# Eight gathered blocks and both edge counts moved into layer 0's first stage

## What is computed

```python
def _gat(x, W, a_src, a_dst, b, src, dst):
    xl = (x @ W).reshape(N, HEADS, C)                    # 4 heads of 32
    al = jnp.einsum('nhc,hc->nh', xl, a_src)
    ar = jnp.einsum('nhc,hc->nh', xl, a_dst)
    e = leaky_relu(al[src] + ar[dst], 0.2)
    m = segment_max(e, dst); w = exp(e - m[dst])
    alpha = w / (segment_sum(w, dst)[dst] + 1e-16)
    return segment_sum(xl[src] * alpha[..., None], dst).reshape(N, HEADS * C) + b

fwd = _gat(layernorm(x), W_f, ..., src, dst)
bwd = _gat(layernorm(x), W_b, ..., dst, src)
```

## Time and profile before

| | |
|---|---|
| median of 3 runs | 5654.59 us |
| the profiled execution | 5651.35 us |
| its span | 5649.4 us |
| instructions | 49583 |
| TensorE busy | 2856.7 us (51%) |
| VectorE busy | 3808.5 us (67%) |
| ScalarE busy | 1462.3 us (26%) |
| GpSimd busy | 3287.9 us (58%) |
| mean granted TensorE clock | 0.73 |

### The profile page before, as it was taken

One profiled execution on the slowest core, in us unless ns is written; L12 is line 12 of the kernel. 1 busy time (PEld: TensorE's weight loads), 2 busy tenths in 40 slices (PEclk: granted clock), 3 DMA queues, 4 the chain that ended last, 5 costly groups with the idle time before them and its releaser, 6 DMA issues. The chain is left out here.

```text
span 5649.4 us, 49583 instructions
## 1 busy us (share of the span) xinstructions
PE 2856.7 (51%) x13052; PEld 2230.7 (39%) x13052; DVE 3808.5 (67%) x6115; ACT 1462.3 (26%) x2526; POOL 3287.9 (58%) x3284
## 2 busy tenths in 40 slices
PE   7513200000000000016799987888888888884777
PEld 5412200000000000015577633777777767773456
DVE  7357778886454555546643464999999998995753
ACT  1113333332233333311222222222222222221220
POOL 0267777777777777754440233777777777772200
PEclk9655555555555555557799998999999999996888
DMA  3133344432363333334232345999999999993114
GB/s 101 36 83 108 102 136 148 132 101 87 103 220 110 110 109 105 106 92 129 87 125 68 101 185 208 314 319 330 322 323 326 321 326 323 322 326 100 67 49 148
DMA packets 288659, 961.78 MB, mean 170 GB/s; under 512 B 77678, under 2 KB 118259, under 8 KB 246896
## 3 DMA queue, kind: packets, MB, share of 16 engines
q0 software_dynamic: 169728, 483.60, 28.1%
q1 hardware_dynamic: 118784, 476.59, 25.4%
HBM read 626.03 MB, written 345.69 MB: 172 GB/s over the span
## 5 line engine op out<-in xcount | busy, mean ns | idle before, releaser
L1249 PE MATMUL e_psE<-e_we,e_eaT 128*128 128x256 f32 x3136 | 899.9, 413 | 268.3 <-DVE e_wv L1148 141.9
L1111 POOL DMA_INDIRECT e_kv<-kv,rec x784 | 875.8, 1117 | 256.1 <-issue 238.2
L779 POOL DMA_INDIRECT g_g<-t,rec x784 | 776.0, 990 | 250.6 <-issue 250.3
L779 POOL DMA_INDIRECT g_g<-t,dst_of x784 | 742.5, 947 | 260.2 <-issue 258.0
L1249 PEld LDWEIGHTS e_psE<-e_we,e_eaT 128*128 128x128 f32 x3136 | 647.1, 209 | 388.9 <-ACT e_eaT L1192 288.5
L1407 PE MATMUL j_psM<-ident,tail 128*128 128x128 f32 x32 | 7.5, 429 | 1148.5 <-PEq L53 1148.5
L1250 PE MATMUL e_psE<-e_kv,ident 128*128 128x256 f32 x1568 | 508.1, 408 | 0.0
L1407 PEld LDWEIGHTS j_psM<-ident,tail 128*128 128x128 f32 x32 | 7.0, 330 | 1149.3 <-issue 1149.3
L816 DVE TENSOR_TENSOR_SCAN g_wv<-g_fx,g_wv 128x2176 f32<-128x2176 f32 x98 | 459.0, 4684 | 0.4 <-issue 0.4
L1118 POOL DMA_INDIRECT e_q<-q,q_of x392 | 370.5, 945 | 119.4 <-issue 119.4
L956 ACT ACTIVATE g_st<-g_wv 128x2048 f32<-128x2048 f32 x98 | 375.8, 3835 | 0.0
(11 more groups left out here) (516 smaller groups left out, 6533.6 us busy)
## 6 DMA issues: line engine op xcount, KB each, us to landing
state<-e_st SPq DMA_DIRECT2D x98, 1088.0 KB, 6.2
e_ea<-in_edge_attr SPq DMA_DIRECT2D x98, 896.0 KB, 9.5
state_f<-g_st SPq DMA_DIRECT2D x49, 1088.0 KB, 4.3
state_b<-g_st SPq DMA_DIRECT2D x49, 1088.0 KB, 4.3
m_work<-xs SPq DMA_DIRECT2D x119, 128.0 KB, 2.2
ys<-m_work SPq DMA_DIRECT2D x119, 128.0 KB, 1.7
xs<-g_ta SPq DMA_DIRECT2D x28, 512.0 KB
g_g<-t,rec POOLq DMA_INDIRECT x784
```

The lines of the kernel that those rows point to most:

```text
L779: pool.indirect_dma_start(g[:, u, j, :], None, tab, bass.IndirectOffsetOnAxis(ap=at_, axis=0)).then_inc(gat[u], 16)
L1111: pool.indirect_dma_start(kv[:, u, b, :], None, c.kv, bass.IndirectOffsetOnAxis(ap=c.rec[:, t, 1:2], axis=0)).then_inc(gkv[u][b // 4], 16)
L1249: nc.tensor.matmul(half, eaT[:, m, j, k, :], we[:, k, :], start=(k == 0), stop=False)
```

## The change

- **First stage.** VectorE's memsets are cut to the padding, and the strip of x is cleared by GpSimd. SyncE loads the weights ahead of x, the attention vectors with four DMAs in place of sixteen, and x in seven column groups with a semaphore each. TensorE folds the weights ahead of the counts; 6 counts go ahead of the tables and 1 lies in each group; 85 follow the tables. Then come 98 counts of the sources (a second bank, `psS`), 54 of them ahead of the work of `target_logits`, which is a helper inside this stage now, and 44 behind it. Both segments' ends are made here (`ends_of(k, ...)`). The records are stored behind the tables.
- **Gathers ahead.** Once the tables are stored, GpSimd gathers the first row per partition and the blocks 0 to 4, then issues the 49 scatters, then gathers blocks 5 to 7. The buffers are a ring of nine: five slots lie in `c.x`, four in `c.gx`.
- **The rank pass** has a reload and regather at its end, under its flag.
- **`graph_passes`** starts at block 8 on GpSimd and waits for a slot nine blocks back. Its counts and segments' ends are gone. The sort's row phases are in blocks 1 to 9, its turns in 10 to 30; SyncE writes and rereads the sorted keys at 34, VectorE unpacks them at 36 and makes the source logits ahead of block 48. The 49 scatters are issued at block 16.
- **`join_tails`** of layer 0 clears the strip of x on GpSimd and reloads x on SyncE, which waits for it.

The diff, cut to its core:

```diff
+RB, RING, RING_X = 16, 9, 5
+EARLY, BEFOREHAND = 5, 8
...
+def ring_slot(c, u):
+    if u < RING_X:
+        return c.x[:, u * (RB * TW):(u + 1) * (RB * TW)].rearrange("p (j w) -> p j w", j=RB)
+    return c.gx[:, u - RING_X]
+def gather_forward(c, pool, blocks, landed_of):
+    for blk in blocks:
+        for j in range(RB):
+            t = blk * RB + j
+            pool.indirect_dma_start(ring_slot(c, blk)[:, j, :], None, c.t1, bass.IndirectOffsetOnAxis(
+                ap=c.key[:, 1, t:t + 1], axis=0)).then_inc(landed_of(blk), 16)
+def target_logits(c, v, landed, first_in, values_in):
+    nc = c.nc
+    nc.vector.tensor_copy(c.lastkey[:, 0:1], c.key[:, 0, T - 1:T])
+    nc.vector.memset(c.sep[:, 0:1], 0.0)
+    nc.vector.tensor_tensor(c.sep[:, 1:T], c.key[:, 0, 1:T], c.key[:, 0, 0:T - 1], ALU.is_equal)
+    v.wait_ge(landed, first_in)
+    v.wait_ge(values_in, 16)
+    nc.vector.tensor_copy(c.ar[:, 0, :], c.first[:, 132:136])
+    v.drain()
+    for h in range(4):
+        nc.vector.tensor_tensor_scan(c.ar[:, :, h], c.sep[:], c.ar[:, :, h], 0.0, ALU.mult, ALU.add)
+    v.drain()
+    nc.vector.tensor_scalar(c.sep[:], c.sep[:], 1.0, BIG, ALU.subtract, ALU.mult)
+    v.drain()
...
-            AHEAD, EACH = 28, 10
-            assert AHEAD + NG * EACH == NBLK
+            names = ("L0_gnn_a_src_f", "L0_gnn_a_dst_f", "L0_gnn_a_src_b", "L0_gnn_a_dst_b")
+            AHEAD, EACH, BEFORE_VALUES = 6, 1, 54
...
+                x = A["x"]
+                rows = x[0:whole, :].rearrange("(p i) d -> p (i d)", i=NI)
+                for g in range(NG):
+                    if g == 3:
+                        sp.wait_ge(padded, 1)
+                    if g == 0:
+                        sp.dma_start(c.x[P - 1:P, 0:pad], x[whole:N, :].rearrange("(p i) d -> p (i d)", p=1)).then_inc(last_x_in, 16)
+                        for at, name in enumerate(names):
+                            with nc.allow_non_contiguous_dma("one word per partition"):
+                                sp.dma_start(avcol[:, at:at + 1], A[name].rearrange("h (c a) -> (h c) a", a=1)).then_inc(av_in, 16)
+                    for p0, p1 in slices_of(0, P - 1):
+                        sp.dma_start(c.x[p0:p1, g * GT * D:(g + 1) * GT * D],
+                                     rows[p0:p1, g * GT * D:(g + 1) * GT * D]).then_inc(x_in[g], 16)
...
+                sp.wait_ge(scattered, 16 * NI)
+                sp.dma_start(c.ar[:], c.st[0][0:EP, :].rearrange("(p t) w -> p t w", p=P)).then_inc(values_in, 16)
+                sp.wait_ge(bd, 2)
+                for q in range(2):
+                    sp.dma_start(c.ends[1][q].rearrange("(p l) -> p l", l=LO), ends[:, 1, q, :]).then_inc(wr, 16)
...
-                nc.vector.memset(key[:], N)
+                nc.vector.memset(key[96:128, :, E - full:T], N)
                 nc.vector.memset(nxt[:], N).then_inc(kz, 1)
-                nc.vector.memset(c.x[96:128, :], 0.0).then_inc(padded, 1)
...
+                v.wait_ge(last_x_in, 16)
+                for g in range(NG):
+                    v.wait_ge(x_in[g], 32)
+                    layernorm_stats(c, v, w, lambda j: c.x[:, (g * GT + j) * D:(g * GT + j + 1) * D], GT, vin, root, g + 1)
+                    if g:
+                        v.wait_ge(tr, g * GT)
+                    for j in range(GT):
+                        nc.vector.tensor_scalar(xln[:, j, 0:D], c.x[:, (g * GT + j) * D:(g * GT + j + 1) * D], w["mv"][:, j, 0:1],
+                                                w["rstd"][:, j:j + 1], ALU.subtract, ALU.mult).then_inc(xr, 1)
+                    for n in counted_with(g):
+                        count(n)
...
+                ends_of(0, psH)
+                for n in range(NBLK, NBLK + BEFORE_VALUES):
+                    count(n)
+                target_logits(c, v, first_in, 16, values_in)
+                for n in range(NBLK + BEFORE_VALUES, 2 * NBLK):
+                    count(n)
...
+                weights()
...
+                pe.wait_ge(vs, 1)
+                nc.tensor.matmul(psV[:, 0:1], c.one[:, 0:1].to_broadcast([P, P]), viol[:, 1:2], start=True, stop=True)
+                for n in rest:
+                    count(n)
+                counted(0, psH)
+                for n in range(NBLK, 2 * NBLK):
+                    count(n)
+                counted(1, psS)
...
+                nc.gpsimd.memset(c.x[96:128, pad:NI * D], 0.0).then_inc(padded, 1)
...
+                pool.wait_ge(kld, 112)
+                pool.wait_ge(stored[0], 32 * (NG // 2 + 1))
+                pool.wait_ge(stored[1], 32 * (NG // 2))
+                c.alone(pool)
+                pool.indirect_dma_start(c.first[:], None, c.t1, bass.IndirectOffsetOnAxis(ap=key[:, 0, 0:1], axis=0)).then_inc(first_in, 16)
+                gather_forward(c, pool, range(EARLY), lambda blk: c.gat[blk])
...
+                gather_forward(c, pool, range(EARLY, BEFOREHAND), lambda blk: c.gat[blk])
...
-        HB, FIRST, TURNS = 6, 18, 27
-        PHASES = ((1, 2, 3), (4,), (5,), (6,), (7,), (8,), (9,), (10,))
+        FIRST, TURNS, KEYS_OUT, SCATTER, COPIES = 1, 10, 34, 16, 18
+        PHASES = ((1, 2), (3,), (4,), (5,), (6,), (7,), (8,), (9,), (10,))
...
+                if 0 <= blk - COPIES < 16:
+                    others += copy_attributes(blk - COPIES)
+                if blk == SCATTER + 4:
+                    sp.wait_ge(scattered, NI * 16)
+                    sp.dma_start(ar_b[:], c.st[1][0:EP, :].rearrange("(p t) w -> p t w", p=P)).then_inc(logits_in, 16)
...
-            for blk in range(NB):
-                u = blk % U
-                if blk == HALF:
+            for blk in range(BEFOREHAND, NB):
+                u = blk % RING
+                if blk == SCATTER:
                     pool.wait_ge(starts_in, 32)
                     c.alone(pool)
                     for i in range(NI):
                         pool.indirect_dma_start(c.st[1], bass.IndirectOffsetOnAxis(ap=startn[:, i:i + 1], axis=0),
                                                 logit[:, i, :], None).then_inc(scattered, 16)
+                if blk == HALF:
                     pool.wait_ge(unpacked, 1)
                     c.alone(pool)
                     pool.indirect_dma_start(first[:], None, c.t2, bass.IndirectOffsetOnAxis(
-                        ap=c.src_of[:, 0:1], axis=0)).then_inc(first_in, 16)
-                if blk >= U:
-                    pool.wait_ge(used, blk - U + 1)
+                        ap=src_of[:, 0:1], axis=0)).then_inc(first_in, 16)
+                if blk >= RING:
+                    pool.wait_ge(used, blk - RING + 1)
                     c.alone(pool)
                 for j in range(G):
                     t = (blk % HALF) * G + j
-                    at_, tab = (c.rec[:, t, 1:2], c.t1) if blk < HALF else (c.dst_of[:, t:t + 1], c.t2)
-                    pool.indirect_dma_start(g[:, u, j, :], None, tab, bass.IndirectOffsetOnAxis(ap=at_, axis=0)).then_inc(gat[u], 16)
+                    at_, tab = (c.key[:, 1, t:t + 1], c.t1) if blk < HALF else (dst_of[:, t:t + 1], c.t2)
+                    pool.indirect_dma_start(ring_slot(c, u)[:, j, :], None, tab,
+                                            bass.IndirectOffsetOnAxis(ap=at_, axis=0)).then_inc(gat[u], 16)
 
         @block.vector
...
+                if blk == KEYS_OUT + 2:
+                    unpack()
+                if blk == HALF - 1:
                     source_logits()
...
+def reload_rows(c, sp, rows_padded, rows_in):
+    x, whole = c.A["x"], (P - 1) * NI
+    sp.wait_ge(rows_padded, 1)
+    for p0, p1 in slices_of(0, P - 1):
+        sp.dma_start(c.x[p0:p1, :], x[p0 * NI:p1 * NI, :].rearrange("(p i) d -> p (i d)", i=NI)).then_inc(rows_in, 16)
+    sp.dma_start(c.x[P - 1:P, 0:(N - whole) * D], x[whole:N, :].rearrange("(p i) d -> p (i d)", p=1)).then_inc(rows_in, 16)
+    sp.wait_ge(rows_in, 48)
...
+            if layer == 0:
+                reload_rows(c, sp, rows_padded, rows_in)
...
+            if layer == 0:
+                pool.drain()
+                nc.gpsimd.memset(c.x[96:128, (N - (P - 1) * NI) * D:NI * D], 0.0).then_inc(rows_padded, 1)
```

More of the change, by code:

```diff
@@ L366, in project @@
                         last.then_inc(mm, 1)
+                weights()
                 for n in range(AHEAD):
                     count(n)
-                weights()
-                pe.wait_ge(vs, 1)
-                nc.tensor.matmul(psV[:, 0:1], c.one[:, 0:1].to_broadcast([P, P]), viol[:, 1:2], start=True, stop=True)
                 for g in range(NG):
@@ L562, in _ @@
                             pool.wait_ge(sct[u], 16 * B * (NBLK // U))
+                        for blk in range(BEFOREHAND):
+                            pool.wait_ge(c.gat[blk], 16 * RB)
+                        pool.wait_ge(rekeyed, 1)
+                        c.alone(pool)
+                        pool.indirect_dma_start(c.first[:], None, c.t1,
+                                                bass.IndirectOffsetOnAxis(ap=key[:, 0, 0:1], axis=0)).then_inc(first_in, 16)
```

(10 more changed lines are left out.)

233 lines of the change are left out of this document (82 added, 151 removed).

## The result

The changed kernel takes 5523.19 us (median of 4 runs, 5517.94 to 5523.34) against 5654.02 for the kernel before in the same comparison (5653.28 to 5657.52). The ratio is 0.9765 with an interval of 0.9748 to 0.9782. Forecast were 5550, with 5520 to 5588 as the range. The profiled execution took 5523.06 us with a span of 5521.3 and a granted clock of 0.73, which is 128.3 us less than the profiled execution before; forecast were 104. So the time lies inside the range, 3 us above its lower end.

What follows compares the result with a forecast made beforehand. GpSimd's 1568 gathers, issued one behind the other, were taken to bound the graph stage. First stage +57, graph stage -168 and -5, join +12 gave -104 us: 5547 profiled, forecast 5550, range 5520 to 5588.

Steps and rivals of the forecast that it cites:

- Rival B: Graph stage, blocks 1 to 30: VectorE becomes the bound, smaller gain; 5626 at 25 us per block, chance 0.03.
- The first stage (+57): Start to the graph stage's first gather: 387.2 instead of 330.14, 57 us longer, bounds +45 and +75.
- Step 1: First stage's start: memset moved to GpSimd, W ahead of x; first statistics at about 23.5 instead of 58.68 us.
- Step 2: First stage's tables: 13.6 us per group, last group out at 124 us, stored and landed at 128.
- Step 3: First stage, GpSimd: 81 gathers and 49 scatters beside counts at 1.36 us each, ending at 308.
- step 4: First stage's values: VectorE waits 27 us until 317, ends done at 381.5; last 48 gathers end at 373, covered.
- The graph stage (-173): Graph stage: 128 gathers leave at 1.31 us, -168; 144 others cheaper by 0.03 each, -5.
- The join (+12): Joining of the tails: strip cleared and x reloaded there, 12 us longer, bounds 0 and +31.
- the 3 us for small transfers beside the load: Join: three rounds of GpSimd's small transfers share the DMA engines with x's reload, adding 3 us.
- case D: Whole kernel: counts don't hamper GpSimd (1.28 per issue), start at 20, reload costs nothing; 5518, chance 0.12.
- Rival A: First stage: GpSimd crawls beside unbroken counts, 2.5 instead of 1.36 us per issue; 5698, slower than before, chance 0.04.
- The rule on tensor_tensor: Issues beside counts: by the skill 130 would cost 0.1 us less each, sum 10 us lower; forecast sided with the rows.

Runs made afterwards that it cites:

- run 2: Changed kernel with four blocks gathered ahead in the first stage instead of eight, ring of nine kept; 5589.41 us, ratio 0.9882.
- run 7: Changed kernel with VectorE clearing x's strip itself and GpSimd's part of the records held until VectorE's copies are done; 5529.18 us, ratio 0.9773.
- run 3: Changed kernel with 77 instead of 54 blocks of the second count ahead of VectorE's wait for the scattered values; 5520.23 us, ratio 0.9759.
- run 12: Kernel before, with each block's gathers counting on one of eight semaphores instead of two; 5618.45 us against 5655.68, ratio 0.9936.
- Run 6: Changed kernel with x reloaded slot by slot as each slot's last block is used up, no 31-row transfer; 5514.34 us, ratio 0.9741.
- run 9: Changed kernel with two buffers, two blocks gathered ahead and gathers counting on eight semaphores in turn; 5648.22 us, ratio 0.9977.
- run 8: Changed kernel with VectorE clearing x's strip, no counts between table groups, earlier square roots, 77 blocks ahead of the values; 5507.48 us, ratio 0.9729.
- run 5: Changed kernel with a ring of two buffers, none in x, and two blocks gathered ahead instead of eight; 5688.49 us, ratio 1.0045.
- run 1: Changed kernel with GpSimd's second-direction wait made shallow, as with two buffers, buffers and semaphores kept; 5527.18 us, ratio 0.9771.
- run 4: Changed kernel with x reloaded at the graph stage's end, 96 partitions early and 31 rows behind a memset; 5570.17 us, ratio 0.9854.

## Why the prediction was right, and where it was off

**The bound was right.** GpSimd's issues set the graph stage's length, ahead and behind: each gather put back lengthened it by 1.33 us (run 2), and VectorE waited for rows only from block 35 on, as forecast. Rival B had no place: the periods of blocks 1 to 31 averaged 18.7 us (18.4 forecast).

**The first stage (+57) was right in its sum, partly by errors that cancel.** Step 1, the start, was 5 us short (28.60 for 23.5). The memset "goes to GpSimd, which is idle" was costed at nothing for VectorE, but its digits, put at 9 to 13 us, were ready at 18: beside the memset and GpSimd's part of the records VectorE's small copies took up to thirteen times as long (run 7). Step 2 was too long: a group takes 12.05 us at a granted clock of 1.00 and over 14 below it, not 13.6. The tables are out at 126.05 for 124, and the first gather is at 130.73 for 128. Step 3's 1.36 us per issue measured 1.35 to 1.40. Step 4's wait of 27 us (29 by its own figures, 317 less 288) measured 25.94. But step 4 took VectorE for the engine that ends the stage and called the last 48 gathers covered. They were not: GpSimd ended it (run 3), 12.67 us of landing and change of stage behind its last gather. The sum came out because VectorE was nearly as late. Its ends were done at 379.0 (378.76 + 0.23); in run 2, where it ended the stage, the next one began 5.5 us behind them (370.52 to 375.98), so here it would have begun at 384.5 instead of 387.1.

**The graph stage (-173) was mis-sized, and this is what made the time lower than the forecast of 5550, by 27 us.** The step that failed is the reading of 0.32 and 0.33 us of idle time per gather as an even price ("3 for its longer pauses", among the first stage's scatters, was all that the forecast gave them). Twelve pauses, 33 us together, lay in that mean, and they went with the two semaphores: run 12 takes them from the kernel before and nothing else, 33.0 us in its trace and 37 by the medians. So about a quarter of the change's 131 us has nothing to do with moving work. Without it the graph stage's -172.7 is the -173 forecast.

**The join (+12) came to +19.7.** The term that failed is the 3 us for small transfers beside the load. They don't run on beside it: in the changed kernel's trace the DMA engines are busy to about 2331 us, the two small gathers land at 2332.7, and all that hangs on them, 14 us, follows only then. That is one wait of 17.61 us for 2.19. Run 6 gives the join's length back.

**That the time fell into the range is in part luck.** The pauses, 33 us, and the join's extra 8 went opposite ways. With the join as forecast the time would have been near 5515, below the range. It lies close to case D's 5518, but none of D's reasons held: the issues beside counts were dearer, the start was at 28.6 and the reload cost more than forecast.

**What the reordering alone costs** follows from runs 9 and 12, both with eight semaphores and two buffers: the new order with two blocks ahead has 0.9977, the old one 0.9936, so the new one is 0.4% or 23 us slower (32 us in the two profiled executions). In the traces the graph stage's first gather of run 9 comes 62.2 us later (392.02 and 329.81, with the wait of 17.29 for a buffer in it) and the join with what follows the last gather is 19 us longer, against 47.4 us less from first to last gather (2403.41 - 392.02 = 2011.39, and 2058.76). The change pays only through the gathers ahead, and with two buffers 17 us of what they save are lost again to that wait.

**Rival A** was wrong where it mattered: beside unbroken counts an issue takes 1.37 to 1.40 us, not 2.5. Undisturbed, a gather takes 1.25, in blocks without counts and sort, and a scatter 1.27 (run 3's stretches). **The rule on tensor_tensor** (the Trainium skill, SBUF — State Buffer, "Who interferes with whom") would have had them at the undisturbed price, since by it a tensor_tensor doesn't meet descriptor generation (the page marks this as inferred). The first stage's 81 gathers ahead of the segments' starts cost 0.12 us more each and its 49 scatters 0.08, some 14 us in all, and run 3 shows that the surcharge comes and goes with the counts. So the trace disagrees with the rule here too.

## What to carry to other kernels

Read the idle time of a group as a distribution before using its mean as a price: one look at the gaps in the timeline would have shown 0.30 us and twelve pauses. Where one engine issues the whole length of a chain through two stages, the start of that chain is worth as much as its body: 21 us came from finishing the tables sooner (run 8), none from filling by itself a 26 us wait of another engine (run 3). A tile lent out as a buffer has to be loaded again somewhere: load it in small pieces as it comes free, in row counts that the 16 engines can share, and not just ahead of a small transfer that the chain waits for.

## What the hardware showed that was not expected

- Gathers that count by turns, in blocks of 16, on two semaphores paused for 2 to 5 us after every 112 of their gathers (at all twelve such places in the kernel before, at eleven of twelve in run 5). On eight semaphores they never did, with the same two buffers (run 9 beside run 5, run 12 beside the kernel before), nor on the changed kernel's nine. How many semaphores are enough wasn't tried; layer 1's six show no pause. What happens in the pause stays open: with nine semaphores a shallow wait doesn't bring it (run 1), and no wait of the kernel's own stands in the rows.
- Beside GpSimd's memset VectorE's cast of 128 x 128 took 3.09 us instead of 0.23, and beside GpSimd's tensor_scalar its shift of 128 x 1568 words 2.32 instead of 0.97 (run 7).
- A load of 31 rows of 49 KB ran at 29 GB/s for over 50 us, with a sixteenth of the DMA engines' time busy; loads of 96, 112, 16 and 15 rows showed nothing of the kind (runs 4 and 6).
- Two gathers of one word per partition, issued behind a load of 6.2 MB on another engine's queue, kept GpSimd waiting for 17.61 us instead of 2.19, until that load was done.
- The seven groups of the tables, with the same work, had from one to three intervals of over 14 us among those of 12.05 (runs 3 and 2). The granted clock was 0.76 or 0.77 in each long one, which cost some 2.5 us of first stage.
